# Message loop of a graph network kernel: fewer TensorE signals, block-diagonal pair weights, later running sums, gathers without waits between them

## What is computed

```python
# first layer, per edge, then per target node
h = concat([x[src], edge_attr])              # 32 + 16 values
h = maximum(h @ w1a + b1a, 0.0)              # 96 values
h = h @ w1b + b1b
agg = segment_sum(h, dst) / maximum(count, 1)
h2 = maximum(concat([x, agg]) @ w2a + b2a, 0.0) @ w2b + b2b
# second layer, ten times
f = 0.9 * (segment_sum((f * src_norm)[src], dst) * dst_norm) + 0.1 * feat0
```

## Time and profile before

| | us |
|---|---|
| three runs | 7000.5, 7002.56, 7007.22 (median 7002.56) |
| span of the profiled execution | 7018.8 |
| message loop in it | about 182 to 2796 |
| of it 254 to 2701, with gathers | 2447 |
| of it 2701 to 2791, no gathers left | 90 |
| propagation and the rest after it | from about 2800 |

### The profile page before, as it was taken

The page is one execution under the profiler, slowest core; times in us unless marked ns, Lnnn a source line. Parts: engine busy times, 40 slices in busy tenths (PEclk is TensorE's granted clock), DMA queues, the critical chain, the costliest instruction groups (busy, mean ns, idle before and its releaser), DMA issues. The chain is left out here.

```text
span 7018.8 us, 211605 instructions
## 1 busy us (share of the span) xinstructions
PE 5576.3 (79%) x85008; PEld 3590.0 (51%) x85008; DVE 4279.1 (61%) x12668; ACT 721.3 (10%) x1695; POOL 1693.3 (24%) x1739
## 2 busy tenths in 40 slices
PE   1455555555555556589999999999999999999998
PEld 1344444444444445446565554656555565656564
DVE  7455555555555557766666666666656666666665
ACT  0122222222222223000000000000000000000000
POOL 5655555555555552500000000000000000000000
PEclk9867676666667767799999999999999999999999
DMA  4322222222222222155545555555555555555554
GB/s 117 77 75 76 76 76 77 75 76 77 79 72 79 72 76 94 27 205 194 200 183 204 192 198 205 189 200 191 201 191 201 191 201 201 189 203 189 197 197 169
DMA packets 442864, 1016.61 MB, mean 145 GB/s; under 512 B 253162, under 2 KB 371914, under 8 KB 387354
## 3 DMA queue, kind: packets, MB, share of 16 engines
q1 hardware_dynamic: 386938, 968.76, 39.0%
q0 software_dynamic: 54944, 33.96, 2.6%
HBM read 838.78 MB, written 176.58 MB: 145 GB/s over the span
## 5 line engine op out<-in xcount | busy, mean ns | idle before, releaser
L1864 PE MATMUL banks_fast<-count_units_fast,feature_parts_fast 128*32 128x512 fp8e3 x70608 | 3826.3, 379 | 31.6 <-DVE count_units_fast L1759 26.9
L1864 PEld LDWEIGHTS banks_fast<-count_units_fast,feature_parts_fast 128*32 128x32 bf16 x70608 | 2146.2, 97 | 1688.5 <-issue 37.5
L1758 DVE TENSOR_SCALAR count_units_fast<-packed_ring_fast 128x512 int32<-128x512 int32 x2949 | 1255.8, 426 | 1429.1 <-PE banks_fast L1864 1398.2
L144 POOL DMA_INDIRECT rows_fast<-row_table,idx_fast x1456 | 1408.5, 967 | 996.9 <-ACT count_stage_fast L1257 563.4
L1759 DVE TENSOR_SCALAR count_units_fast<-packed_ring_fast 128x512 int32<-128x512 int32 x2949 | 1237.2, 420 | 0.0
L1351 PE MATMUL banks_fast<-w1a_b1a_fast,turn_fast 49*128 49x96 f32 x3136 | 374.6, 375 | 810.6 <-ACT turn_fast L1262 589.6
L1223 DVE TENSOR_SCALAR window_place_hot_fast<-iota_wide_fast,local_keys_fast,target_weight_fast 128x196 bf16<-128x196 f16 x3136 | 933.9, 343 | 0.0
L1316 PE MATMUL banks_fast<-window_place_hot_fast,window_src_hot_fast 128*128 128x196 bf16 x3136 | 697.4, 312 | 115.4 <-issue 71.0
L1322 PE MATMUL banks_fast<-window_place_hot_fast,window_src_hot_fast 128*128 128x196 bf16 x3136 | 680.2, 305 | 106.1 <-issue 105.4
L1351 PEld LDWEIGHTS banks_fast<-w1a_b1a_fast,turn_fast 49*128 49x128 f32 x3136 | 294.9, 260 | 917.4 <-issue 497.4
L1316 PEld LDWEIGHTS banks_fast<-window_place_hot_fast,window_src_hot_fast 128*128 128x128 bf16 x3136 | 410.1, 155 | 224.2 <-issue 148.3
(11 more groups left out here) (282 smaller groups left out, 1551.5 us busy)
## 6 DMA issues: line engine op xcount, KB each, us to landing
packed_ring_fast<-edge_counts SPq DMA_DIRECT2D x422, 1792.0 KB, 7.0
edge_counts<-count_stage_fast SPq DMA_DIRECT2D x100, 784.0 KB
running_sums<-run_sums_fast SPq DMA_DIRECT2D x100, 768.0 KB
rows_fast<-row_table,idx_fast POOLq DMA_INDIRECT x1456
rows_fast<-attrs_padded SPq DMA_DIRECT2D x98, 128.0 KB
attrs_padded<-in_edge_attr SPq DMA_DIRECT2D x1, 12500.0 KB
rows_fast<-row_table,src_ends_fast POOLq DMA_INDIRECT x112
row_table<-h_nodes_fast SPq DMA_DIRECT2D x1, 1568.0 KB, 5.2
```

The source lines that it names most:

```text
L144: pool.indirect_dma_start(out=self.rows[:, r, c, 0:DN], out_offset=None, in_=b.dram.table, in_offset=bass.IndirectOffsetOnAxis(ap=idx[:, c ...
L1758: nc.vector.tensor_scalar(to[..., 0:P // 8], of, NIBBLES, None, ALU.bitwise_and)
L1864: last = nc.tensor.matmul(b.banks[at:at + DN, SWEEP[m % 2], 0:COLS], parts[:, side, j, k * DN:(k + 1) * DN], of_strip.bitcast(FP8), start= ...
```

## The change

1. **TensorE signals.** mix(q) and turn(q + 1) share one signal (`mixed_and_turned`), and all counts of a quarter share one (`quarter_counted`): 8 a group. The key signal is gone too, since the keys ride on `mixed_and_turned`.
2. **Pair weights.** `w_pair` has `w1a` twice on a block diagonal. mix(q) is two matmuls with 128 rows and 192 output columns for four with 49 rows and 96 columns.
3. **Running sums.** The adds of a quarter are done three quarters later (`LAG`), four in each quarter, one after every second one-hot tile.
4. **Gathers.** POOL issues the 16 gathers of a group with no wait between them. It still waits for the last transpose of group g before the gathers of group g + 7.
5. ACT copies the keys out of PSUM (`keep_keys`); its order becomes copy(q + 1), Relu(q), two casts with one signal.

```diff
+    LEAD = SLOTS * Q
+        turned_keys = sb("turned_keys", [P, 2, LW])
+        w_pair = sb("w1a_of_pairs", [P, 2, DH])
-        T_BANK, S_BANK, M_BANK, C_BANK = 0, 1, 2, (4, 5, 6, 7)
+        T_BANK, S_BANK, M_BANK, C_BANK = 0, 1, (2, 3), (4, 5, 6, 7)
+        LAG = 3
...
-                pool.wait_ge(turned, (SLOTS + g + 1) * Q)
+                pool.wait_ge(mixed_and_turned, g * Q + (LEAD + Q))
...
-                for u in range(READS):
-                    if u:
-                        pool.wait_ge(count_read, (SLOTS + g + 1) * READS - READS // Q + u)
-                        pool.sem_inc(taken, 1)
-                    ahead.gather(pool, b, r, idx[:, r, :], range(u * G // READS, (u + 1) * G // READS))
+                ahead.gather(pool, b, r, idx[:, r, :], range(G))
...
-                        dve.wait_ge(hot_used, g * (WG // 2) + (q + 1) * (QW // 2))
-                        if q == Q // 2:
+                        dve.wait_ge(quarter_counted, g * Q + (q + 1))
+                        if q == 1:
...
-                            if q * QW + w < G:
-                                add_run(1 - s, g, q * QW + w)
+                            if w % 2:
+                                if w == 1:
+                                    dve.wait_ge(mix_read, g * Q + (q + 1))
+                                add_run((s + back) % SLOTS, g + back, of_quarter * QC + w // 2)
...
+                    for q in range(Q):
+                        act.wait_ge(mixed_and_turned, g * Q + (LEAD + 2 + q))
+                        if q == KEYS_Q and s == SLOTS - 1:
+                            keep_keys()
+                        keep_turned((q + 1) % 2)
+                        if q == 0:
+                            act.wait_ge(sums_out[s], (k + 1) * 16)
+                        nc.scalar.activation(sums[:, s, q * QC:(q + 1) * QC, :], ...
+                                             ACT.Relu).then_inc(mix_read, 1)
+                        act.wait_ge(quarter_counted, g * Q + (q + 3))
+                        for u in (2 * q, 2 * q + 1):
+                            kept = nc.scalar.copy(to, of)
+                        kept.then_inc(count_read, 1)
...
+                for q in range(Q):
+                    pe.wait_ge(turn_read, g * Q + (q + 1))
+                    pe.wait_ge(mix_read, g * Q + (q + LAG - 1))
+                    last = mix(q)
+                    if q < Q - 1:
+                        last = turn_rows(r_rows, q + 1)
+                    elif not is_last:
+                        pe.wait_ge(gathered[after % AHEAD_GROUPS], (turns + 1) * (G * 16))
+                        last = turn_rows(after % AHEAD_GROUPS, 0)
+                    last.then_inc(mixed_and_turned, 1)
+                    pe.wait_ge(count_read, g * Q + (q + LEAD - 1))
+                    for r in range(q * (QW // 2), (q + 1) * (QW // 2)):
+                        last = count(r)
+                    last.then_inc(quarter_counted, 1)
```

More of the change, by code:

```diff
@@ L1063, in messages_and_counts @@
         KEY_STEPS, RUN_STEPS = 6, G + 1
-        READS = WG // 4
-        FILLS = 12
+        LAG = 3
+        FILLS = 15
         @block.gpsimd
@@ L1292, in turn_keys, with turn_rows @@
                                             b.ident[:, 0:LW], start=True, stop=True, skip_group_check=True)
-                last.then_inc(keys_turned, 1)
+                return last
+            def turn_rows(r, q):
+                for k in range(QC // 2):
+                    c = q * QC + 2 * k
+                    last = nc.tensor.transpose(b.banks[:, T_BANK, k * P:(k + 1) * P],
+                                               rows[:, r, c:c + 2, :].rearrange("p c d -> p (c d)"), b.ident[:, :])
+                return last
@@ new lines, in _, with group, mix, count @@
+            pe.wait_ge(gathered[0], G * 16)
+            pe.wait_ge(attrs_in[0], 16)
+            turn_rows(0, 0).then_inc(mixed_and_turned, 1)
+            def group(i, t):
+                g, s, r_rows = i * BATCH + t, t % SLOTS, t % AHEAD_GROUPS
+                after = t + 1
+                turns = i * (BATCH // AHEAD_GROUPS) + after // AHEAD_GROUPS
+                is_last = isinstance(g, int) and g == J - 1
+                def mix(q):
+                    for k in range(QC // 2):
+                        last = nc.tensor.matmul(b.banks[:, M_BANK[q % 2], k * 2 * DH:(k + 1) * 2 * DH], turn[:, q % 2, k * P:(k + 1) * P],
+                                                w_pair[:, :, :].rearrange("p o d -> p (o d)"), start=True, stop=True, skip_group_check=True)
+                    return last
+                def count(r):
+                    m = (r // (QW // 2)) % 2
+                    pe.wait_ge(hot, SLOTS * WG + g * WG + 2 * (r + 1))
+                    u, side = divmod(r, 2)
+                    for half in range(2):
+                        w = (2 * r + half) % QW
+                        nc.tensor.matmul(b.banks[:, C_BANK[u % 4], side * WC:(side + 1) * WC], part_hot[:, m, :, w],
+                                         place_hot[:, m, w, :], start=(half == 0), stop=(half == 1))
+                    for half in range(2):
+                        w = (2 * r + half) % QW
+                        last = nc.tensor.matmul(b.banks[:, S_BANK, half * WC:(half + 1) * WC], part_hot[:, m, :, w],
+                                                place_hot[:, m, w, :], start=False, stop=False, skip_group_check=True)
+                    return last
+                for q in range(Q):
+                    pe.wait_ge(turn_read, g * Q + (q + 1))
+                    pe.wait_ge(mix_read, g * Q + (q + LAG - 1))
+                    if q == KEYS_Q and s == SLOTS - 1 and not (isinstance(g, int) and g >= J - 2):
+                        next_keys = t // SLOTS + 1
+                        pe.wait_ge(keys_in[next_keys % AHEAD_GROUPS], (i + next_keys // AHEAD_GROUPS + 1) * 16)
+                        turn_keys(next_keys % AHEAD_GROUPS)
+                    last = mix(q)
[3 more added lines that the diff above has]
+                        pe.wait_ge(gathered[after % AHEAD_GROUPS], (turns + 1) * (G * 16))
+                        pe.wait_ge(attrs_in[after % AHEAD_GROUPS], (turns + 1) * 16)
+                        last = turn_rows(after % AHEAD_GROUPS, 0)
[4 more added lines that the diff above has]
+                    last.then_inc(quarter_counted, 1)
@@ L1365, in _ @@
+            with pe.Fori(0, n_loops - 1) as i:
+                for t in range(BATCH):
+                    group(i, t)
+            for t in range(BATCH):
+                group(n_loops - 1, t)
             nc.tensor.matmul(b.banks[:, S_BANK, 0:P], b.zeros16[:, :], b.zeros16[:, :], start=False, stop=True,
```

149 lines of the change are left out of this document (45 added, 104 removed).

## The result

The changed kernel takes **7157.85 us** (7141.2 to 7162.0, 4 runs) against 7002.81 for the kernel before (4 runs): ratio 1.0218, 95% interval 1.0204 to 1.0232. It is slower, where 6775 us were forecast. The profiled execution spans 7155.0 us, against 7018.8 before. So the spans differ by 136 us and the medians by 155; what follows accounts for the 136.

The account below looks back on a forecast made before the run. No engine was full; the gather stream, delaying TensorE's signals, was taken to bound the message loop. Savings 217 + 4 + 7 + 1 - 1 = 228 us off 7018.8 gave span 6791, so 6775 us; range 6450 to 7090.

Parts of the forecast that it names:

- the period: Message loop, time per group with gathers: 26.89 us before, forecast 24.5 us, saving 217 us over 91 groups.
- the lateness L: Message loop: delay of a TensorE signal while gathers run, put between 3.9 and 8.8 us.
- the middle case: Message loop: L grows from 3.9 to 8.8 us within a run of gathers, giving a period of 25.0 us.
- the third arrives only after POOL stops: Case L = 8.8 us throughout: third signal of a group comes at 20.6 plus 1.1 us, the next sent at 23.7.
- my upper end of 27.4: Message loop period in us with L = 8.8 throughout; by this end the change loses 46 us.
- a little under the middle one: Choice of 24.5 us from periods 22.0, 25.0 and 27.4, because runs of 13 gathers showed 3.9 us.
- Can go either way: Pauses of POOL that let signals through, 2.1 a group before, one possible after; gather runs 20.6 us for about 9.
- Gathers at 20.6 us a group: POOL in the message loop: sixteen gathers of 1.25 us and half a key fetch (0.6), taken for the changed loop too.
- VectorE is caught too: Rival, chance 0.22: VectorE's own signals turn late in long gather runs; period 28.5 us, 7137 us.
- POOL becomes the bound: Rival, chance 0.18: TensorE is never late for POOL, gathers run on at 20.7 us a group; 6420 us.
- Nothing gained: Rival, chance 0.14: L stays 8.8, fewer signals and fewer pauses cancel; period 26.5 to 27.4, 6990 to 7035 us.
- The Trainium skill's rule: Matmul completion signals serialize at some 26 ns each: 28 signals would be 0.74 us a group, 72 us; set aside.

Follow-up runs that it names:

- The square: Pauses put back into the changed kernel, 6973 us, and taken out of the kernel before, 7427 us, beside those two kernels at 7158 and 7003 us.
- 128x320: Changed kernel with a 128x320 f32 filler memset of POOL behind each gather of the loop: 6851.1 us, ratio 0.9770 to the kernel before.

## Why the prediction was wrong

**The step that failed is the period, and in it the lateness L.** It was taken between 3.9 and 8.8 us and the period at 24.5. In the group shown above the signals are 0.1, 5.0, 11.8 and 0.1 us late. They are sent 1.7, 4.0, 11.7 and 26.2 us after POOL's start, where the middle case had 3.7, 9.6, 20.4 and 25. So the first three come earlier than forecast, and then the third isn't up to 8.8 us late but is used only when POOL has stopped. L doesn't end at 8.8: most signals sent late in a run wait for its end, by 11.8, 16.1 or 19.6 us in the rows above. The 8.8 us of the earlier trace rows, alike in neighbouring batches, comes from another stage with one signal a batch, and I used it as an upper bound for this loop.

I had the case "the third arrives only after POOL stops" in my upper end of 27.4. That end plus the longer gathers (0.85) is 28.2, measured 28.13, but so close a match is partly luck. That end had two quarters after the stop; in the group shown there is one, and its parts are longer. The run lasts 21.7 us, the signal is used 1.8 us after it, copies up to the next mix take 0.7, mix and transposes 2.1, and POOL starts 1.4 us after they end (1234.92), 27.65 us in all. The choice "a little under the middle one", on the strength of one signal in a run of 13 gathers, was thus the error: 28.13 - 24.5 = 3.6 us a group, 330 us, of which the longer gathers are 77.

**Pauses.** "Can go either way" was the right warning, but they got no price of their own. The square gives it: 185 us. A saving of 217 us was forecast for the loop; the rest of the change, with pauses in place, brings 30 (59 without the loss in the propagation stage).

**Gathers at 20.6 us a group** were taken over unchanged. They took 0.85 us more, 77 us in all. With tile and add by turns they shorten, so VectorE's new order does it; why is open. It isn't a pure loss, since the shorter gathers were worse.

**The rivals.** The time, 7158, lies near that of "VectorE is caught too" (7137), but its mechanism didn't occur: it asked for VectorE's waits on its own signals of 500 us; adds waited 0.4 us for adds, and VectorE's idle time lies before its wide tile, which waits for TensorE's counts. From its waits in 400 to 2500 us:

```profile
DVE window_src_hot_fast L1220 <- remote: 665.3, 85, 26.8
...
DVE run_sums_fast L1186 <- DVE run_sums_fast L1186: 0.4, 1, 0.4
```

"POOL becomes the bound" is what happens once the gathers are spaced, at 2100 / (1309 / 16) = 25.7 us a group with 128x320, not at 20.7. "Nothing gained" was the nearest in mechanism, with too low an end. Two bounds don't follow from the prediction's own sum: a period of 22.2 us gives about 6560 us, not 6530, and one of 26.5 about 6960, not 6990. Neither bears on the outcome.

**The Trainium skill's rule** (page "TensorE: Matmul & The Clock Gate", section "The cost: per-tile semaphore tail") of some 26 ns a signal: no run here agrees while gathers are dense. Without pauses the loop with 28 signals fewer was 3.2 us a group shorter (28.13 for 31.37 us between the stores; the other parts of the change are in this too), for 0.74 by the rule, and lateness reached 19.6 us. With gathers 1.7 us apart the number was worth nothing, which doesn't contradict it.

**Small terms.** Pair weights were put at nothing, on equal column counts; they cost about 15 us, since two wide matmuls took 0.84 us and the four narrow ones 0.69. Groups without gathers 14.56 us for the 14.3 forecast (3 us saved for 4). Start: the first gather of the loop came at 238.81 us instead of 248.90, yet the first stores only 1.6 us earlier. The clock with gathers was unchanged, as argued. Adds and SP's later stores: hidden, as argued. Not foreseen at all: 29 us in the propagation stage. In sum: 113 + 29 - 3 (groups without gathers) - 3 (start and between the stages) = 136 us.

## What to carry to other kernels

When one engine issues indirect DMAs back to back, look at the time from the end of a TensorE instruction to the start of what waits for it, by its age in the run; if it grows, that engine's idle time can be the effect of its own density, and rests by time or a little filler between the gathers can be worth more than the waits removed. Price a removed wait as a loss too: what flowed during it. And give the case in which a late signal comes only when the disturbance stops a chance of its own; here it was the common one.

## What the runs showed of the hardware

- Filler on POOL made the loop faster: gathers 1.32 us apart 7158 us, 1.54 apart 6851, 1.70 apart 7072. TensorE's signals are late by 16.1 and 19.6 us in rows of the dense stream and by 1.9 us at most with 1.70. VectorE's adds aren't late in the group shown, and ACT's signal isn't either: a copy ends at 1216.65, 9.4 us into the run, and TensorE goes on at 1216.89. What they queue for no run shows.
- At 1.48 us of spacing the same kernel ran at 0.980 and, on another chip, 0.997 of the kernel before.
- A gather (about 0.94 us with VectorE idle) gets longer beside VectorE's new order: mean 1020 ns for 967; with tile and add by turns 976.
- More instructions of TensorE ahead of an untouched stage changed that stage from 4013 to 3972 us; its idle times with nothing to wait for of 5 us went away.
